# A graph network's edge stage: Relu before the attributes' split, padding not gathered, and a reordered preparation

## What is computed

```python
h = jnp.maximum(_layernorm(x, axis=-1), 0.0)
e = jax.nn.relu(ea @ ee_w1 + ee_b1) @ ee_w2 + ee_b2
msg = x[src] + e
agg = jax.ops.segment_sum(msg, dst, num_segments=n)
h = (1.0 + eps) * x + agg
```

## Time and profile before

| | |
|---|---|
| median of three runs | 3133.91 us |
| profiled execution, its own time | 3134.97 us |
| its span (first to last instruction) | 3133.0 us |
| busy: PE / DVE / ACT / POOL | 2456.0 / 2233.0 / 1592.6 / 1984.4 us |
| mean granted TensorE clock | 0.903 |
| HBM read / written | 346.95 / 25.80 MB |

### The profile page before, as it was taken

One profiled execution on the slowest core, in us unless ns is written; L12 is line 12 of the kernel. 1 busy time (PEld: TensorE's weight loads), 2 busy tenths in 40 slices (PEclk: granted clock), 3 DMA queues, 4 the chain that ended last, 5 costly groups with the idle time before them and its releaser, 6 DMA issues. The chain is left out here.

```text
span 3133.0 us, 88320 instructions
## 1 busy us (share of the span) xinstructions
PE 2456.0 (78%) x29338; PEld 2164.5 (69%) x29339; DVE 2233.0 (71%) x3932; ACT 1592.6 (51%) x3967; POOL 1984.4 (63%) x2094
## 2 busy tenths in 40 slices
PE   2677677777777779999999999938777777777773
PEld 2566666666666679999999999936555555555652
DVE  6566667776777657777777777758777777777777
ACT  6555555555555558888888888821111111111114
POOL 5677767777777724454544444437777777777772
PEclk9988889888899989999999999969888888988896
DMA  7555555555555510000000000026555555555554
GB/s 168 165 152 160 152 147 159 164 162 160 158 157 160 148 45 17 23 20 21 23 20 21 20 23 20 23 77 178 172 173 170 171 174 174 167 174 172 172 171 135
DMA packets 183986, 373.55 MB, mean 119 GB/s; under 512 B 42741, under 2 KB 93959, under 8 KB 183912
## 3 DMA queue, kind: packets, MB, share of 16 engines
q0 software_dynamic: 75552, 209.45, 23.7%
q1 hardware_dynamic: 107392, 162.37, 17.2%
q10 hardware_dynamic: 968, 0.87, 0.1%
HBM read 346.95 MB, written 25.80 MB: 119 GB/s over the span
## 5 line engine op out<-in xcount | busy, mean ns | idle before, releaser
L550 POOL DMA_INDIRECT rows<-tab_scratch,srcs x784 | 750.7, 958 | 264.4 <-issue 229.3
L1561 POOL DMA_INDIRECT a_rows<-tab_scratch,srcs x784 | 751.7, 959 | 250.9 <-issue 226.7
L1627 PE MATMUL sum_ps<-feat,a_hot 128*125 128x264 f32 x1960 | 599.0, 462 | 207.1 <-DVE feat L1720 98.1
L1627 PEld LDWEIGHTS sum_ps<-feat,a_hot 128*125 128x125 f32 x1960 | 417.6, 222 | 310.3 <-issue 117.8
L979 PE MATMUL z_ps<-ah,w 128*128 128x125 f16 x6400 | 555.1, 219 | 2.7 <-PEq L1075 2.6
L979 PE MATMUL z_ps<-al,w 128*128 128x125 f16 x3200 | 544.1, 218 | 0.0
L979 PEld LDWEIGHTS z_ps<-ah,w 128*128 128x128 f16 x6400 | 490.8, 97 | 3.5 <-issue 3.4
L1571 ACT ACTIVATE feat<-d 128x32 f32<-128x32 f32 x196 | 44.9, 229 | 827.2 <-DVE d L1716 580.5
L626 PE MATMUL sum_ps<-hot,rows 128*128 128x125 f16 x1960 | 356.1, 235 | 53.0 <-PEq L642 24.6
L612 PE MATMUL mlp_ps<-ewa,eab 128*128 128x256 f16 x788 | 213.9, 301 | 229.6 <-PEq L608 229.1
L626 PE MATMUL sum_ps<-hot,rh 128*128 128x125 f16 x1960 | 354.4, 234 | 0.0
(11 more groups left out here) (220 smaller groups left out, 5938.7 us busy)
## 6 DMA issues: line engine op xcount, KB each, us to landing
ea<-edge_t SPq DMA_DIRECT2D x394, 128.0 KB
dstb<-dst_flat SPq DMA_DIRECT2D x98, 512.0 KB, 4.0
rows<-tab_scratch,srcs POOLq DMA_INDIRECT x784
a_rows<-tab_scratch,srcs POOLq DMA_INDIRECT x784
tab_scratch<-prow SPq DMA_DIRECT2D x50, 128.9 KB
hx<-x SPq DMA_DIRECT2D x50, 125.0 KB
x_scratch<-x SPq DMA_DIRECT2D x50, 125.0 KB
hs<-tab_scratch SPq DMA_DIRECT2D x50, 125.0 KB
```

The costliest lines, as they stand in the source:

```text
L550: pool.indirect_dma_start(rows[:, b % DEEP, k, :], None, dram["tab0"], bass.IndirectOffsetOnAxis(ap=srcs[:, c:c + 1], axis=0),).then_inc(r ...
L1561: pool.indirect_dma_start(rows[:, b % DEEP, k, :], None, dram["tab1"], bass.IndirectOffsetOnAxis(ap=srcs[:, c:c + 1], axis=0),).then_inc(r ...
L1627: ins = pe.matmul(out[:], hot[:, h, k, :], feat[:, row, k, :], start=(k == 0), stop=(k == CB - 1))
```

## The change

In `prepare`: `tb` gets 9 buffers, a view of the weights' room `w`; chunk 9 uses the first again. `own_factors` and `numbers` run ahead of the first `stats`. The extremes are made one reduction at a time in steps 3 to 6 and the schedule in steps 7 and 8; SP stores it behind chunk 6's rows. The last chunk's bias addition moves from POOL to VectorE (`last_sum`). `own` and `deviation` change places, and so do VectorE's `own`, `low` and `stats`.

In `edges0`: ScalarE makes the Relu of batch b ahead of `high_parts` of b+1, and `eah` after `high_ps`; VectorE makes `low_activations` ahead of `low_parts` in both branches, and both ahead of `add` where there is a second tile. In both edge stages the two columns that hold only padding are not gathered.

```diff
+FILLED = -(-E // P)
...
-        TB = 3
+        LASTC = CH - 1
+        TB = CH - 1
+        extra_fills = (3, 4, 5, 6)
-        tb = m.sb("tb", [TN, TB, PG, 2 * D], F16)
+        tb = sb["w"][:].rearrange("p r q h -> p (r q h)")[0:TN, 0:TB * PG * 2 * D].rearrange(...)
...
-            for c in range(CH - 1):
-                store(c)
-            sp.wait_ge(sched_ready, 1)
...
-            store(CH - 1)
+            for c in range(CH):
+                store(c)
+                if c == LASTC - 3:
+                    store_schedule()
...
-            for c in range(CH):
+            for c in range(LASTC):
                 pool.wait_ge(norm_ready, c + 1)
...
                 if c >= 3:
-                    own(c - 3)
+                    own(c - 3, (1,) if on_act(c - 3) else (0,))
                 if c + 1 < CH:
                     deviation(c + 1)
+                if c >= 3 and on_act(c - 3):
+                    own(c - 3, (0,))
...
+            def last_sum():
+                dve.wait_ge(ld_b2, 16)
+                dve.wait_ge(norm_ready, CH)
+                dve.tensor_tensor(ht[:, LASTC % 2], acc[0:TN, tiles(LASTC), 0:D], b2bc[:]..., ALU.add).then_inc(t_last, 1)
...
             dve.sem_inc(consts, 1)
+            numbers()
+            own_factors()
             stats(0)
             for c in range(CH + 3):
                 if c < CH:
                     coefficients(c)
-                if 3 <= c < CH:
-                    own(c - 3)
+                if c == CH:
+                    last_sum()
                 if 2 <= c < CH + 2:
                     low(c - 2)
...
                 if c + 1 < CH:
                     stats(c + 1)
-                if c == 0:
-                    own_factors()
-                if c == 1:
-                    numbers()
+                if c >= 3:
+                    own(c - 3)
```

```diff
 def high_parts(s):
     act.activation(eab[:, s, :], ea[:, s, :], ACT.Copy).then_inc(eab_chain, 1)
-    act.activation(eah[0:ED, s, :], ea[0:ED, s, :], ACT.Copy).then_inc(eah_done, 1)
     act.wait_ge(mlp_free, 1)
...
     act.activation(high_ps[s], eab[ED:P, s, :], ACT.Copy).then_inc(ea_high, 1)
+    act.activation(eah[0:ED, s, :], ea[0:ED, s, :], ACT.Copy).then_inc(eah_done, 1)
...
     for u in range(RING):
         s = u % 2
-        high_parts(1 - s)
         act.wait_ge(mlp_done, 1)
...
         act.activation(rh[:, s]..., mlp_ps[:, s]..., ACT.Relu).then_inc(r_high, 1)
+        high_parts(1 - s)
...
     with dve.If(end > lo + 1):
         extra_hot(b - 1, end - 1)
+        low_activations(s)
+        low_parts(1 - s)
         add(1 - s, lo)
-        low_parts(1 - s)
-        low_activations(s)
         main_hot(b + 1, 1 - s, following)
...
     with dve.Else():
+        low_activations(s)
         low_parts(1 - s)
-        low_activations(s)
         add(1 - s, lo)
...
-    for k in range(CB):
+    for k in range(min(CB, FILLED - CB * b)):
```

More of the change, by code:

```diff
@@ L165, in prepare @@
         own_kept = [m.sem(f"own_kept{j}") for j in range(KD)]
-        tb_stored = [m.sem(f"tb_stored{s}") for s in range(TB)]
+        first_stored, tb_stored, t_last = m.sem("first_stored"), m.sem("tb_stored"), m.sem("t_last")
         dve_chain = m.sem("p_dve_chain")
@@ L197, in store, with store_schedule @@
                 for rows in splits:
-                    sp.dma_start(tb_v[rows, tiles(c), :], tb[rows, c % TB]).then_inc(tb_stored[c % TB], 16)
-            for c in range(CH - 1):
-                store(c)
-            sp.wait_ge(sched_ready, 1)
[L203 to L208, removed]
-            store(CH - 1)
+                    sp.dma_start(tb_v[rows, tiles(c), :], tb[rows, c % TB]).then_inc(tb_stored if c else first_stored, 16)
+            def store_schedule():
+                sp.wait_ge(sched_ready, 1)
+                sp.dma_start(dram["spans"][1:NBP + 1].rearrange("(p j) c -> p (j c)", j=2), spans_sb[:].rearrange("p j c -> p (j c)")).then_inc(stored, 16)
+                sp.dma_start(dram["spans"][0:1], spans_sb[0:1, 0, :]).then_inc(stored, 16)
+                for p in range(2):
+                    line = dram["sched"][p]
+                    sp.dma_start(line[1:NBP + 1].rearrange("(p j) -> p j", j=2), sched_sb[:, p, :]).then_inc(stored, 16)
+                    sp.dma_start(line[0:1].unsqueeze(0), sched_sb[0:1, p, 0:1]).then_inc(stored, 16)
+            for c in range(CH):
+                store(c)
+                if c == LASTC - 3:
+                    store_schedule()
             sp.wait_ge(stored, 112)
-            for s in range(TB):
-                sp.wait_ge(tb_stored[s], 32 * len(range(s, CH, TB)))
+            sp.wait_ge(tb_stored, 32 * LASTC)
         @block.gpsimd
@@ L261, in high, with own @@
                 act.activation(tb[:, c % TB, :, 0:D], ht[:, c % 2], ACT.Copy).then_inc(hi_ready, 1)
-            def own(c):
+            def own(c, parts):
                 if c == 0:
                     act.wait_ge(own_coef, 1)
-                for j in range(KD) if on_act(c) else (0,):
+                for j in parts:
                     act.wait_ge(own_done[j], c + 1)
@@ L348, in low, with extreme @@
                 dve.sem_inc(t_free, 1)
-            def extremes(j):
+            def last_sum():
+                dve.wait_ge(ld_b2, 16)
+                dve.wait_ge(norm_ready, CH)
+                dve.tensor_tensor(ht[:, LASTC % 2], acc[0:TN, tiles(LASTC), 0:D], b2bc[:].unsqueeze(1).broadcast_to([TN, PG, D]),
+                                  ALU.add).then_inc(t_last, 1)
+            def extreme(q):
                 dve.wait_ge(ld_dst, 16)
-                dve.tensor_reduce(ext[:, j:j + 1], drow[:, j, :], AX, ALU.min)
-                settled(dve.tensor_reduce(ext[:, 2 + j:3 + j], drow[:, j, :], AX, ALU.max))
+                settled(dve.tensor_reduce(ext[:, q:q + 1], drow[:, q % 2, :], AX, ALU.min if q < 2 else ALU.max))
             def numbers():
@@ L374, in own_offset, with passed @@
                 dve.sem_inc(own_coef, 1)
-            def schedule():
+            def passed():
                 settled(dve.tensor_tensor(cmp_[:], ext[:].unsqueeze(2).broadcast_to([half, 4, NT - 1]),
@@ L379, in schedule @@
                 settled(dve.tensor_reduce(tile[:], cmp_[:], AX, ALU.add))
+            def schedule():
                 settled(dve.tensor_copy(sched_sb[:, 0, :], tile[:, 0:2]))
@@ L389, in _ @@
                     coefficients(c)
[L390 to L391 removed]
+                if c == CH:
+                    last_sum()
                 if 2 <= c < CH + 2:
                     low(c - 2)
[L394 to L397, removed]
[L398 to L406 removed]
+                if c == 5:
                     dve.wait_ge(eb_high, 1)
@@ L409, in _ @@
                     dve.sem_inc(eb_split, 1)
-                if c == CH:
+                if c + 1 < CH:
+                    stats(c + 1)
+                if c >= 3:
+                    own(c - 3)
+                if c == 2:
+                    own_offset()
+                if c in extra_fills:
+                    extreme(c - extra_fills[0])
+                if c == CH - 3:
+                    passed()
+                if c == CH - 2:
                     schedule()
@@ L633, in _, with body @@
             edge_mlp(0)
-            def body(tiles, i, u):
+            def body(tiles, i, u, last=False):
                 s = u % 2
@@ L657, in _ @@
             for u in range(REST):
-                body(tiles, FULL, u)
+                body(tiles, FULL, u, u == REST - 1)
         @block.vector
```

14 lines of the change are left out of this document (9 added, 5 removed).

## The result

The changed kernel takes 3243.22 us (median of four runs, 3242.78 to 3247.21) against 3133.25 (four runs of the kernel before): ratio 1.0355, 95% interval 1.0337 to 1.0373. It is slower, by 110 us where 87 were forecast.

| stage, us | before | after | difference | forecast |
|---|---|---|---|---|
| preparation, to VectorE's first step of the edge stage | 89.1 | 81.6 | -7.5 | -5 |
| first edge stage, to POOL's first step behind it | 1033.1 | 1148.4 | +115.3 | +94 |
| node stage, to the second edge stage's first gather | 967.4 | 967.0 | -0.4 | 0 |
| second edge stage and finish | 1043.4 | 1044.6 | +1.2 | -2 |
| span | 3133.0 | 3241.6 | +108.6 | +87 |

The account below looks back on a forecast made before the run. No engine was busy throughout; POOL's 5.03 us a batch and the consumers' 5.21 lay close. First edge stage +94, preparation -5 and second edge stage -2 on 3134.97 gave 3222, as median 3221 us; range 3120 to 3285.

Parts of the forecast that it names:

- The ring: First edge stage: each plain batch becomes a closed loop over ScalarE, VectorE and TensorE without lead, 4.85 us, 946 for 195.
- Loop ends and rows: First edge stage: delays at TensorE's loop ends 49 us, weight rows 48, VectorE's loop ends 18, both loop ends together -11.
- The clock: First edge stage: MLP matmuls at 1.2 instead of 2.4 GHz, half the earlier share, add 17 us, bounds 0 and 35.
- two-tile batches: First edge stage: 49 batches of two tiles take 0.84 us over the plain 4.85, 41 us in all.
- the ring as summed: Main case: the terms of the first edge stage hold as added; ends 3158 and 3285 us; 79%.
- Preparation: Stage before the edges: new order and moved stores against memsets holding conversions, sum -5 us, bounds -14 and +2.
- step (a): Preparation: own_factors and numbers leave the path of chunks 1 and 2 before the first stats, -7.4 us.
- what was put at 3: Preparation's end: last addition goes to VectorE, six schedule stores leave SP's queue before the last table store, -3 us.
- Second edge stage: Second edge stage: last batch has 2 gathers instead of 4 and starts sooner, -2 us, bounds 0 and -2.5.
- POOL's pace decides: First edge stage: consumers' mean falls under POOL's 5.03 us a batch, so gathers set the time, 3087 us; 8%.
- Losses and gains: First edge stage: losses on plain batches and gains on the others cancel, 5.21 us stays, 3127 in all; 9%.
- The lower clock throughout: First edge stage: TensorE stays at 1.2 GHz throughout, +139 us, 3360 in all; 4%.

## Why the prediction was right, and where its sum was off

**The ring: right.** What was to show it is there: ScalarE's wait before nearly every Relu (1.8, forecast 2), POOL waiting over 100 us, the first statistics at 14.18, Relus no closer than 4.67 (4.7). The order alone makes the loss, the ring has no slack (the 0.43 put in came out in full), and either swap closes it. One sign was weaker than forecast: POOL waited 152 us in all, but before 74 gathers, in some 70 of the 196 batches and not in most. The ring was taken 0.18 too long: eab starts 0.92 after the Relu and high_ps 0.74 after eab (102.17, 103.09, 103.83), where 1.03 and 0.82 were taken; all other members came within 0.04 of what was taken. That is 195 x 0.18 = 35 less than the forecast's 946.

**Loop ends and rows: right.** 49 were taken for TensorE's loop ends, less 11 for both at once; 51 went with them. A weight row was put at 4.4: the row that begins at 674.85 has a period of 9.79, which is 4.67 + 4.30 and 0.82 of a slow MLP. VectorE's loop end behind a batch of two tiles: 2.2 on average in the six that meet nothing else, 1.9 in the three of them without a slow MLP, for 1.66.

**The clock: wrong.** The step was "The gaps become shorter, so I take half that share", 17 us, at most 35. The gaps became longer (TensorE's idle time before the MLP grew from 230 to 351 us) and the mean fell from 0.89 to 0.84, so there was nothing to halve. TensorE in order of time, the first MLP matmul of a quiet batch, behind TensorE's loop end and behind a weight row; then windows of TensorE alone (duration, busy time, granted clock, DMA share, GB/s), two of the three MLPs, and the sums ahead of a second tile's in two batches:

```profile
105.58 0.27 PE L628 MATMUL mlp_ps<-ewa,eab 128*128 128x256 f16 x1 [1.83 <-PEq L624]
...
268.92 0.37 PE L628 MATMUL mlp_ps<-ewa,eab 128*128 128x256 f16 x1 [3.32 <-PEq L624]
...
682.57 0.37 PE L628 MATMUL mlp_ps<-ewa,eab 128*128 128x256 f16 x1 [5.31 <-PEq L624]
```

```profile
682.60:684.20 1.60, 1.60 (x8) 0.50 0.39 101
105.60:106.60 1.00, 1.00 (x11) 1.00 0.47 131
...
734.76:736.52 1.76, 1.76 (x34) 1.00 0.81 206
776.95:780.26 3.31, 3.31 (x33) 0.50 0.59 186
```

After 1.83 idle the MLP runs at 2.4 GHz and takes 1.05; after 5.31 it runs at 1.2 GHz and takes 1.87. Over the stage 64 of 197 MLPs took more than 1.2 us (51 before), and what they took over 1.05 adds up to 40 us. They are commoner behind long waits: 29 of the 40 MLPs with the longest idle time before them are slow. But the other 157 hold 35 of them and nearly half of the 40 us. The prediction's own measure would have served with the right clock and no halving: at 0.84, 32% of the stage is at 1.2 GHz, and 0.32 x 195 x 0.8 is 50. In a batch of two tiles the sums ahead of it count as well:

```profile
735.12 1.02 ACT L602 ACTIVATE rh<-mlp_ps 128x1024 f16<-128x1024 f32 x1 [1.78 <-ACTq L601]
...
740.74 1.02 ACT L602 ACTIVATE rh<-mlp_ps 128x1024 f16<-128x1024 f32 x1 [2.71 <-ACTq L601]
...
777.36 1.03 ACT L602 ACTIVATE rh<-mlp_ps 128x1024 f16<-128x1024 f32 x1 [6.90 <-ACTq L601]
...
783.72 1.02 ACT L602 ACTIVATE rh<-mlp_ps 128x1024 f16<-128x1024 f32 x1 [3.44 <-ACTq L601]
```

5.62 at the higher level, 6.36 at the lower. Of the 34 such batches outside loop ends 17 took 5.61 to 5.63 (0.95 over the plain period, for a forecast 0.84) and the others up to 6.92, 10 us in all. So the clock's price here is some 50 and not 17. It is added up from rows, not shown by taking it away: the one attempt to raise the clock took 5 of the 40 away and lost more elsewhere. The Trainium skill, "TensorE: Matmul & The Clock Gate", section "HAM oscillation — how this bites in real kernels", describes such a cost, each burst of matmuls behind a wait starting cold. The rows agree for 29 of the 40 MLPs with the longest idle time before them and show slow ones behind shorter waits too. The prediction, which named the section for a rival, could have used it for this term.

**The rest of the 22.** -35 of the ring, +33 of the clock and +5 of the two-tile batches leave some 19 us, among them the 11 taken off for coincidences. By batch, with slow MLPs and the usual 0.95 of a second tile taken out, some 6 of the 19 lie in batches of two tiles with VectorE's loop end, which were put at nothing, some 6 in batches of one tile with that loop end or none, and some 4 in the weight rows. That the ring's 35 too much and the clock's 33 too little nearly cancel is luck.

**The range.** The lower end of the ring as summed does not follow from its terms: no hop is 43, no self-wait 37 and a third of the row and loop delays 32, together 112 and not 63, which would put it at 3109 instead of 3158. The measured time lies far above both.

**Preparation: right in sign, its parts less so.** The memsets hold the conversions, first statistics at 14.18 (forecast 14.6). The Trainium skill, "SBUF — State Buffer", section "SBUF: two separate sides", says that of a GpSimd operation and a VectorE operation that needs the shared ports, one holds them for its whole instruction. The rows agree, and the experiment without memsets at the start shows it: 10.80 against 0.23. By the stages the preparation gained 7.5 with first statistics 5.4 later. But that 5.4 was not all on the path, as the sum took it: with the factors behind the first statistics only 2.3 of the earlier start reached chunk 3. Of the wait before ScalarE's normalisations 9.1 of the 13.0 is left, so step (a) brought 3.9 and not 7.4. By these figures what was put at 3, the end with the last addition on VectorE and the schedule's stores moved, brought between 6 and 9, an estimate; no run took these apart.

**Second edge stage: no gain that can be told.** Its last batch waited 0.64 for its rows, not 1.62: 1 us of the 2.

```profile
3192.33 0.19 DVE L1728 TENSOR_TENSOR e<-a_rows,ht_ps 128x32 f32<-128x32 f32 x1 [0.64 <-DVEq L1522]
```

The stage with the finish took between 1041.5 and 1044.8 in the thirteen profiles, whatever the kernel, which hides that.

**The rivals.** POOL's pace decides only without the ring (5.2 us of waiting). Losses and gains did not cancel. The lower clock throughout did not come; at 0.84 it is nearer than at 0.89.

## What to carry to other kernels

Before moving a step ahead of another on one engine, follow one item round through all engines and ask on which of them the next item's step is still issued first. Here one engine alone that put this item's step first was enough: the lead was gone, stalls that the lead had hidden came back, and the period became the sum of the members. An order that helps the rare batch (here the one of two tiles) can be changed in that branch alone. And the share of slow clock is to be forecast for the loop as it will idle, not as it idled before.

## What the runs showed of the hardware that was not expected

A VectorE conversion of 0.23 issued 0.1 after POOL's first memset did not come in between that memset and the next, queued behind it: it waited through both, 10.80. Reading twelve schedule registers at once cost TensorE a gap of 3.3 us in the ring's path, while two at a time cost nothing that the period shows. The schedule's conversion to int32, 0.17 in the kernel before, took 3.56 beside POOL's addition and memset pieces and ended with them.
